# Layer 1 of a two-layer attention and expert kernel: values and routed rows go through the result bank, and both transposed results are one item

## The reference, cut to what matters

```
x = x + cross_attention_0(layernorm(x), ctx, Wq, bq, Wk, bk, Wv, bv, Wo, bo)   # with rotary positions
x = x + experts_0(layernorm(x))                                                # every token, top 8 of 64 experts
x = x + cross_attention_1(layernorm(x), ctx, Wq, bq, Wk, bk, Wv, bv)           # no positions, no output product
x = x + experts_1(layernorm(x))                                                # top 8 of 64, capacity per expert
```

## Time and profile before

| | us |
|---|---|
| median of 3 runs | 2026.81 |
| lowest, highest | 2024.23, 2028.75 |
| the profiled execution | 2026.57 |
| its span, first to last instruction | 2024.9 |
| PE / DVE / ACT / POOL busy, share of the span | 81% / 70% / 61% / 49% |

### The profile page before, as it was taken

How to read it: one execution, slowest core, us unless ns; L and a number is a source line. 1 busy time by engine, 2 the same in 40 slices (tenths; PEclk the granted TensorE clock), 3 DMA queues, 4 the chain that set the end, 5 groups by cost and what they waited for, 6 DMA issues and landing times. The chain is left out here.

```text
span 2024.9 us, 44338 instructions
## 1 busy us (share of the span) xinstructions
PE 1633.4 (81%) x12470; PEld 1095.1 (54%) x12623; DVE 1412.4 (70%) x4341; ACT 1236.0 (61%) x3174; POOL 989.1 (49%) x1114
## 2 busy tenths in 40 slices
PE   3999999999965999999997378888888888855551
PEld 1555555555534888998886134444444444444430
DVE  5888899999954455554434589999999999743330
ACT  1777777777752566666664378778778777621110
POOL 4367777777772000000001776666666662158883
PEclk9999999999987999999998699999999999969995
DMA  5689888787757966666665678887777785178756
GB/s 139 170 211 246 240 220 221 220 220 220 213 169 219 293 202 201 199 203 194 198 197 161 171 191 220 231 219 194 201 198 191 198 199 144 43 200 188 174 94 110
DMA packets 413085, 390.94 MB, mean 193 GB/s; under 512 B 46640, under 2 KB 385072, under 8 KB 412848
## 3 DMA queue, kind: packets, MB, share of 16 engines
q1 hardware_dynamic: 346496, 265.28, 49.4%
q0 software_dynamic: 37904, 90.22, 16.8%
q10 hardware_dynamic: 28448, 32.59, 5.6%
HBM read 233.74 MB, written 170.16 MB: 199 GB/s over the span
## 5 line engine op out<-in xcount | busy, mean ns | idle before, releaser
L1131 DVE TENSOR_REDUCE mx<-psS 128x2 f32<-128x512 f32 x1024 | 678.1, 677 | 88.1 <-PE psS L1525 60.2
L929 ACT ACTIVATE prob<-psE 128x512 f32<-128x512 f32 x1024 | 592.9, 593 | 220.3 <-PE psE L1538 202.5
L778 POOL DMA_INDIRECT yg<-y_d,row_all x256 | 249.5, 975 | 627.5 <-SPq L417 478.6
L1538 PE MATMUL psE<-q,k 128*128 128x256 bf16 x2048 | 393.1, 274 | 35.9 <-ACT prob L929 12.5
L1525 PE MATMUL psS<-k,q 128*128 128x512 bf16 x871 | 336.0, 387 | 28.8 <-DVE mx L1131 14.5
L1477 DVE TENSOR_TENSOR hid<-sil,psE 128x96 f32<-128x96 f32 x384 | 97.7, 254 | 330.5 <-ACT sil L1030 330.5
L1658 PE MATMUL psE<-wt,xgT 128*128 (+1 forms) x1536 | 324.0, 334 | 1.2 <-ACT xgT L1025 0.4
L765 POOL DMA_INDIRECT xs_d<-xr,row_all x256 | 252.1, 985 | 119.9 <-ACT prob L929 75.3
L1538 PEld LDWEIGHTS psE<-q,k 128*128 128x128 bf16 x2048 | 187.3, 98 | 187.4 <-ACT prob L929 59.4
L1556 PE MATMUL psO<-prob,v 128*32 128x256 f32 x4096 | 274.1, 385 | 0.0
L1025 ACT COPY xgT<-psS 128x256 f32<-128x256 f32 x384 | 144.5, 376 | 185.9 <-PE psS L1652 159.6
(11 more groups left out here) (222 smaller groups left out, 2523.8 us busy)
## 6 DMA issues: line engine op xcount, KB each, us to landing
xg<-xs_d SPq DMA_DIRECT2D x320, 128.0 KB, 2.5
y_d<-y_all SPq DMA_DIRECT2D x320, 128.0 KB, 2.3
q<-q_stack_d SPq DMA_DIRECT2D x128, 256.0 KB
k<-k_stack_d SPq DMA_DIRECT2D x128, 256.0 KB
wt<-in_gu ACTq DMA_DIRECT2D x110, 192.0 KB, 3.1
q_stack_d<-parts SPq DMA_DIRECT2D x64, 192.0 KB
k_stack_d<-parts SPq DMA_DIRECT2D x64, 192.0 KB
wt<-in_dn ACTq DMA_DIRECT2D x110, 96.0 KB, 3.8
```

Of the source, the lines that this page charges most:

```text
L778: g.indirect_dma_start(yg[:, k, :], None, y0_d[:, :], bass.IndirectOffsetOnAxis(row_all[:, row(st.pair("load") * K + k, 1)], 0))\
L929: a.activation(prob[gr][:, u % 4, :], psE[ring][:, :], ACT.Exp, scale=SCALE).then_inc(s_exp, 1)
L1131: v_.tensor_reduce(mx[b][:, bg // 4, :].rearrange("p (h r) -> p h r", h=2)[:, :, (bg % 4) * 2 + tt], psS[(UNITS * (st.s0 - LAG["smax"]) + ...
L1538: ins = m_.matmul(psE[ring][:, i * T:(i + 1) * T], k2[b][:, bg, hh * T + i * P:hh * T + (i + 1) * P], q2[b][:, bg, :], start=True, stop=True)
```

## The change

The table of layer 1 gets a third bank, number 2, which is the result bank psO. V and XT move to it; K moves from bank 1 to bank 0, LG from bank 0 to bank 1; OT0 and OT1 become one item OT of four transposes in bank 1, as layer 0 has it. Layer 0's table stays.

In layer 1 these move between units: V on TensorE from 3 to 4; K from 4 to 5; XT from 10 to 5; OT from 5 and 6 to 6; NT from 8 to 9; mT0 from 9 to 10. On ScalarE xr goes from 8 to 4, the copy of XT from 11 to 5, the high part of mT0 from 9 to 10. On VectorE both reciprocals stand in unit 6 and both normalising products in unit 7, the sum x1 goes from 8 to 9, the low part of mT0 from 10 to 11. An item on psO waits until both halves of the result before have been copied out (semaphore s_oev), and the first `values` product of a step waits until V and XT have been copied out of psO (s_v, s_xT).

```diff
@@ MISC, layer 1
-    (("mT1", "attn", 0), ("RK", "place", 1), ("V", "smax", 0), ("K", "front", 1), ("OT0", "back", 0),
-     ("OT1", "back", 1), ("Q", "front", 0), ("NT", "back", 1), ("mT0", "smax", 0), ("XT", "route", 1),
-     ("LG", "route", 0), ("LIST", "post", 1)),
+    (("mT1", "attn", 0), ("RK", "place", 1), ("V", "smax", 2), ("K", "front", 0), ("XT", "route", 2),
+     ("OT", "back", 1), ("Q", "front", 0), ("NT", "back", 1), ("mT0", "smax", 0), ("LG", "route", 1),
+     ("LIST", "post", 1)),
...
@@ bank
-            return psM[at]
+            if at == 2 and st.on("back"):
+                pe.wait_ge(s_oev, st.n("back", 2))
+            return small[at]
+
+        small = [*psM, psO]
...
@@ ScalarE
-                    if u == (10, 11)[L] and st.on("route"):
+                    if u == (10, 5)[L] and st.on("route"):
...
-                    if u == (10, 9)[L] and st.on("smax"):
+                    if u == 10 and st.on("smax"):
                         max_rows("smax", 0)
-                    if u == (14 if filled else (4, 6)[L]) and (st.on("front") or st.on("route")):
+                    if u == (14 if filled else 4) and (st.on("front") or st.on("route")):
                         act.wait_ge(s_rstd, 4 * st.roots())
...
-                    if u == (6, 8)[L] and st.on("route"):
+                    if u == (6, 4)[L] and st.on("route"):
...
@@ VectorE
-                    if L == 1 and u == 8 and st.on("back"):
+                    if L == 1 and u == 9 and st.on("back"):
...
-                    if u == (11, 10)[L] and st.on("smax") and not filled:
+                    if u == 11 and st.on("smax") and not filled:
                         split_max("smax", 0)
...
-                    if u == (7, 5)[L] and st.on("back"):
+                    if u == (7, 6)[L] and st.on("back"):
                         invert(0)
-                    if u == (7, 6)[L] and st.on("back"):
-                        if L == 0:
-                            invert(1)
+                        invert(1)
+                    if u == 7 and st.on("back"):
                         normalise(0)
-                        if L == 1:
-                            invert(1)
-                    if u == 7 and st.on("back"):
                         normalise(1)
...
@@ TensorE, values
+                    if st.L == 1 and q == 0:
+                        if st.on("smax"):
+                            pe.wait_ge(s_v, st.n("smax"))
+                        if st.on("route"):
+                            pe.wait_ge(s_xT, st.n("route"))
...
@@ TensorE, units
-                    if u == 4 and st.on("front"):
+                    if u == (3, 4)[L] and st.on("smax"):
+                        b = st.buf("smax")
+                        product("V", "smax", [(d_ctx[b], st.nbuf("smax"))],
+                                [(ctx_t[b][:, i * P:(i + 1) * P], wbd[L]["v"][:, :]) for i in range(2)], s_vp, P)
+                    if u == (4, 5)[L] and st.on("front"):
                         b = st.buf("front")
                         product("K", "front", [(d_ctx[b], st.nbuf("front"))],
                                 [(wbd[L][n][:, :], ctx_t[b][:, :]) for n in ("ks", "k")[L]], s_kp)
-                    if u == 3 and st.on("smax"):
...
+                    if L == 1 and u == 5 and st.on("route"):
+                        rows_of_x(st)
+                    if u == 6 and st.on("back"):
                         pe.wait_ge(s_oev, st.n("back", 2))
                         ps = bank(pe, st, "OT")
...
-                    if L == 1 and u in (5, 6) and st.on("back"):
-                        h = u - 5
-                        product(f"OT{h}", "back", [(s_oev, st.n("back", 2))],
-                                [(osb[:, half, h * P:(h + 1) * P], None) for half in range(HALVES)], s_ot[h])
-                    if u == (9, 8)[L] and st.on("back"):
+                    if u == 9 and st.on("back"):
                         product("NT", "back", [(s_nrm[0], st.n("back")), (s_nrm[1], st.n("back"))],
                                 [(nrm[:, h, :], None) for h in range(2)], s_ntp)
-                    if u == (10, 9)[L] and st.on("smax"):
+                    if u == 10 and st.on("smax"):
                         product("mT0", "smax", [(s_max, st.n("smax", UNITS, 8))],
                                 [(mx[st.buf("smax")][:, 0, :], None)], s_mT[0])
```

More of the change, by code:

```diff
@@ L438, in lastbuf @@
             return st.nbuf(stage, per) - per
-        FREE = dict(mT0=s_mlo[0], mT1=s_mlo[1], V=s_v, OT=s_nrm[1], OT0=s_nrm[0], OT1=s_nrm[1], Q=s_qr, K=s_kr,
+        FREE = dict(mT0=s_mlo[0], mT1=s_mlo[1], V=s_v, OT=s_nrm[1], Q=s_qr, K=s_kr,
                     NT=s_nt, WO=s_x1, XT=s_xT, LG=s_logit, RK=s_tot, LIST=s_list)
@@ L465, in head_cols @@
         def head_cols(L, h, o, n):
-            tile = psM[item_bank(L, ("OT", f"OT{h}")[L])]
-            first = (h, 0)[L] * 2 * P
+            tile = small[item_bank(L, "OT")]
+            first = h * 2 * P
             return tile[:, first:first + 2 * P].rearrange("p (h r) -> p h r", r=HALF)[:, :, o:o + n]
@@ L915, in max_rows @@
                         act.wait_ge(d_max[h][before.buf(stage)], before.nbuf(stage, 32))
-                    a.copy(mhi[h][:, :], psM[item_bank(L, f"mT{h}")][0:16, 0:P]).then_inc(s_mhi[h], 1)
+                    a.copy(mhi[h][:, :], small[item_bank(L, f"mT{h}")][0:16, 0:P]).then_inc(s_mhi[h], 1)
                 filled = L == 1 and st.s0 == FULL - 2
@@ L940, in body @@
                         wait(act, s_rem, last(st, "front", back=NB))
-                        ps = psE[0] if filled and i == 0 else psM[item_bank(1, "QK"[i])]
+                        ps = psE[0] if filled and i == 0 else small[item_bank(1, "QK"[i])]
                         a.activation(qk[b][:, i, :], ps[:, 0:T], ACT.Identity,
@@ L951, in body @@
                         wait(act, s_wo, last(st, "back"))
-                        a.activation(nt[:, :], psM[item_bank(0, "NT")][:, 0:T], ACT.Identity,
+                        a.activation(nt[:, :], small[item_bank(0, "NT")][:, 0:T], ACT.Identity,
                                      bias=bias[:, 7:8]).then_inc(s_nt, 1)
@@ L998, in body @@
                         wait(act, s_ex, last(st, "route"))
-                        a.copy(logit[:, :], psM[item_bank(L, "LG")][:, 0:E]).then_inc(s_logit, 1)
+                        a.copy(logit[:, :], small[item_bank(L, "LG")][:, 0:E]).then_inc(s_logit, 1)
                     if u == (15 if filled else 13) and st.on("front"):
@@ L1137, in split_max @@
                     dve.wait_ge(s_mhi[h], st.n(stage))
-                    v_.tensor_tensor(mlo[h][:, :], psM[item_bank(L, f"mT{h}")][0:16, 0:P], mhi[h][:, :], ALU.subtract)\
+                    v_.tensor_tensor(mlo[h][:, :], small[item_bank(L, f"mT{h}")][0:16, 0:P], mhi[h][:, :], ALU.subtract)\
                       .then_inc(s_mlo[h], 1)
                 def invert(h):
-                    dve.wait_ge(s_ot[1 if L == 0 else h], st.n("back"))
+                    dve.wait_ge(s_ot[1], st.n("back"))
                     ch.add(v_.reciprocal(rec[:, h, :], head_cols(L, h, 8, 1).rearrange("p h o -> p (h o)")), f"rec{h}")
@@ L1157, in rotate @@
                     b = st.buf("front")
-                    ps = psM[item_bank(0, "QK"[i])]
+                    ps = small[item_bank(0, "QK"[i])]
                     dve.wait_ge((s_qp, s_kp)[i], st.n("front"))
@@ L1222, in body @@
                         now, left = (tally[(st.s0 - LAG["place"] + i) % 2] for i in range(2))
-                        v_.tensor_tensor(now[:, :, :], psM[item_bank(L, "RK")][:, 0:2 * E].rearrange("p (h e) -> p h e", h=2),
+                        v_.tensor_tensor(now[:, :, :], small[item_bank(L, "RK")][:, 0:2 * E].rearrange("p (h e) -> p h e", h=2),
                                          left[:, 1:2, :].broadcast_to((P, 2, E)), ALU.add).then_inc(s_tot, 1)
@@ L1309, in body @@
                         wait(dve, d_x1[b], lastbuf(st, "back"))
-                        v_.scalar_tensor_tensor(x1[b][:, :], psM[item_bank(0, "WO")][:, 0:T], bias[:, 4:5], xres[b][:, :],
+                        v_.scalar_tensor_tensor(x1[b][:, :], small[item_bank(0, "WO")][:, 0:T], bias[:, 4:5], xres[b][:, :],
                                                 ALU.add, ALU.add).then_inc(s_x1, 1)
                     if L == 1 and u == 15 and st.on("post"):
-                        ps = psM[item_bank(1, "LIST")]
+                        ps = small[item_bank(1, "LIST")]
                         dve.wait_ge(s_lsp, st.n1("post"))
@@ L1572, in product, with rows_of_x @@
                     ins.then_inc(done, 1)
+                def rows_of_x(st):
+                    b = st.buf("route")
+                    product("XT", "route", [(s_xr, st.n("route"))],
+                            [(xr[b][:, i * P:(i + 1) * P], None) for i in range(2)], s_xtp)
                 def q_rows(st):
@@ L1600, in body @@
                                 [(wbd[L][n][:, :], ctx_t[b][:, :]) for n in ("ks", "k")[L]], s_kp)
```

(12 more changed lines are left out.)

10 lines of the change are left out of this document (3 added, 7 removed).

## The result

| | before | changed |
|---|---|---|
| median | 2027.78 us (4 runs) | 2005.49 us (4 runs) |
| lowest, highest | 2024.23, 2032.04 | 2001.72, 2007.01 |
| the profiled execution | 2026.57 | 2007.01 |
| its span | 2024.9 | 2005.3 |

The ratio is 0.9886, 95% interval 0.9862 to 0.9911: 22 us faster by the medians, 19.6 between the two profiled executions, where 25.8 were forecast. The time of 2005.5 lies 4.5 us above the 2001 of the forecast. The same kernel beside a second set of runs (experiment 8) gave 0.9891, 0.9876 to 0.9905.

What follows compares the result with a forecast made beforehand. VectorE was taken as the bound, with only its idle time before the reductions of units 4 and 8 to win. 2026.6 - 27.0 - 1.5 + 2.7 = 2000.8, forecast as 2001 us; range 1994 to 2018.

Steps and rivals of the forecast that it cites:

- The two stalls, 27.0 us: VectorE's waits before the reductions of units 4 and 8 go: 1.00 us a step in 27 steps, 27.0 us.
- 49 of 50: Sign that the forecast is right: VectorE busy 49 of 50 us in a window of attention 1.
- The split: Gain per step by stall: 0.37 us before the reduction of unit 4, 0.63 before that of unit 8.
- Fill and drain, -1.5 us: Filling and emptying steps of attention 1: 1.5 us won of the 5.8 us of waits there.
- second stalls: VectorE's 0.55 us wait before the reduction of unit 8, in steps 6 to 32, expected to go.
- what is late next at unit 5: V behind ScalarE's copy of the result delays the scores of unit 5, but they stay covered by 0.3 us.
- rival D: VectorE's stalls only move, to units 5 and 6, so nothing is won: 2024 to 2029 us; chance 0.06.
- The new stall at unit 8, +2.7 us: Q waits for a later xn, delaying the reduction of unit 8: 0.1 us a step, bounds 0 and 0.2.
- The store, 0: Storing mlo costs nothing: about 3.1 us left, landing taken near 2.1; bounds 0 and 0.6 us a step.
- rival A: The store of mlo becomes the new wait, 0.5 to 0.6 us a step lost: about 2016 us; chance 0.15.
- Rivals A, B and C: Rival A; B: the unit 8 stall stays, about 2015 us, 0.08; C: store landing 5.6 us after issue, 2065 us, 0.06.

Runs made afterwards that it cites:

- experiment 8: The changed kernel itself run again beside a second set of runs of the kernel before: 2006.59 us, ratio 0.9891.
- experiment 1: Kernel before with only V moved, to unit 4 and psO: 2021.86 us, ratio 0.9969. Its marks: low part in unit 3 of step 7 to step 9.
- experiment 4: Changed kernel with mT0, and so the store of the low part, one unit earlier on all three engines: 2006.03 us, ratio 0.9899.
- OT alone: Kernel before with only OT0 and OT1 made one item OT, reciprocals in unit 6, products in unit 7: 2013.70 us, ratio 0.9935.
- experiment 3: Kernel before with V on psO in unit 4 and one item OT, but XT and xr left where they were: 2010.07 us, ratio 0.9909.
- experiment 7: Changed kernel with mT0, and so the store of the low part, two units later except in the last filled step: 2017.95 us, ratio 0.9959.
- experiments 3 to 6: Experiment 3, experiment 4, the changed kernel with V one unit later (2008.96 us), and that with mT0 one unit earlier as well (2008.78 us).

## Why the prediction was right, point by point

*The two stalls, 27.0 us.* Right in mechanism and size. Undisturbed steps went from 19.08 to between 18.06 and 18.11 us, VectorE to 99.6% where 49 of 50 was named, and experiments 1 to 3 show the two waits apart. The split was off: 0.37 and 0.63 were foreseen, alone they gave 0.28 and 0.46, and the rest only together.

*Fill and drain, -1.5 us.* This is the term that failed. The emptying steps gave 2.2 us, about what was asked of them. The filling stretch was to get shorter, by its share of this term and by three of the 27 second stalls (1.9 us); it took 96.95 and 96.82 us in two traces, against 95.38 in the one of before. Of the 6.2 us missing between the profiled executions, 3 to 5 are here. The step at fault is the one on what is late next at unit 5: its cover of 0.3 us was worked out in a full step and taken for all. In step 7 VectorE has fewer instructions (no tally stands before the reduction of unit 4), reaches the reduction of unit 5 sooner, and stands 1.01 us for it:

```profile
1208.98 0.69 DVE L1135 TENSOR_REDUCE mx<-psS 128x2 f32<-128x512 f32 x1 [1.01 <-PE psS L1525]
```

Step 8 has the same, 0.98 us. Steps 7 and 8 by the marks of experiment 1 show whose it is, since they come again within 0.03 us in three traces with V and XT where the change puts them (33.29, 33.31, 33.32; experiments 4 and 8 are two of them):

| kernel | steps 7 and 8, us | the filling stretch ahead of them, us |
|---|---|---|
| before | 32.60 | 62.78 |
| V alone | 34.78 | 65.56 |
| OT alone | 31.49 | 65.05 |
| changed | 33.29, 33.32 | 63.66, 63.50 |

OT's part won its two second stalls, V's part cost 1.8 to 2.2 us. That was rival D's mechanism, at unit 5, in the place where its condition held. The cost is the change's own for 0.7 of the 1.5 us. The rest lies ahead, where OT alone took 2.3 us longer with V unmoved, and where the changed kernel was 0.67 us behind by step 5 already, when no V waits for osb yet; this rest is not explained, and with one usable trace of before it can be chance.

*The new stall at unit 8, +2.7 us.* Did not come. From the tally, xn ended 3.19 us later (1409.27 to 1412.46), where the forecast had 3.75 (1413.10 to 1416.85). ScalarE was 0.35 us ahead at osb already (0.67 us before the tally, 0.32 in the earlier trace rows), where I had allowed up to 0.2. In experiment 3, with xr and XT in their later units, it was 0.43 us before the tally, so 0.24 of this is their move.

*The store, 0.* Right: no scores of either trace of the changed kernel wait for it. In most steady steps it lands 1.7 us after its issue (experiment 7) and not at the 2.1 taken from a larger store; the 3.1 us left were more than enough. In 11 steps of experiments 3 to 6, and in crowded ones of experiment 7, scores waited until 2.8 to 4.5 us after the issue, so rival A's mechanism exists, but only the delay of experiment 7 made it cost time that could be seen. The rule of the Trainium skill that was weighed ("DMA: Bandwidth & Descriptors", "Queues, rings and completion order") is borne out by no run: it would fit the crowded steps, but weight loads from ScalarE are under way there too, and none sets the two apart. Rivals A, B and C are out as forecasts for the whole stage.

*Steps 13 to 15.* They lost 2.7 us more than before in the first trace and 1.9 in the second, a cost that the forecast has no term for. In the first, step 13 lost 1.0 us behind a late ScalarE (experiment 4), step 14 lost 0.8 by a mask that waited for GpSimd (below), and step 15 lost 1.6. There two reductions stood 0.54 and 0.55 us for scores, in a stretch in which TensorE's granted clock fell from 1.00 (1349 to 1351 us) to a mean of 0.54 (1351 to 1353) and 0.61 (to 1355), most of it at the lower level, 1.2 GHz; `values` took 1.88 us for 1.07. TensorE had been busy 1.04 of the 2.00 us before. In the second trace the clock stayed at 1.00 and step 15 lost 1.8 us, 0.91 of it at the reduction of unit 5 behind V and 0.5 in the long hotr. That is rival D's mechanism again: where ScalarE's copy comes late, V behind it makes the reduction of unit 5 late. The missing stall of unit 8 made good for most of this.

## What to carry to other kernels

When the engine that sets the end waits for another, which waits for it, take that wait off and price it by the idle time in the bracket: 0.84 of the 1.00 us was that. A cause is not read from a bracket alone: the one of 2.71 us named TensorE, and it was ScalarE's own issue. Count the cover of a moved wait separately in steps that are only half filled and in steps where the engine that is waited for now can be late: a cover worked out in an undisturbed full step is not there. A gain read from one trace holds for its condition: where TensorE's results came 1.4 us later, a kernel with this change was no faster than before.

## What the runs showed of the hardware

An instruction of VectorE with two operands in SBUF that started while GpSimd ran its product of 128x512 on SBUF ended only after it. The mask, 0.23 us otherwise, in the changed kernel:

```profile
1348.00 1.15 POOL L828 TENSOR_TENSOR parts<-rem,parts 128x512 bf16<-128x512 f32 x1 [0.73 <-ACT parts L1007]
...
1348.21 1.02 DVE L1351 TENSOR_TENSOR mask<-rest,logit 128x64 bf16<-128x64 f32 x1
```

It ends at 1349.23, the product at 1349.15. The same befell the sums ys (1.53 for 0.67 us), x (0.91 for 0.40) and hotr (1.71 for 1.22), in each of six traces at one or more places. With an operand in PSUM, or one operand only, nothing happens, in the kernel before for instance:

```profile
1406.95 1.17 POOL L824 TENSOR_TENSOR parts<-rem,parts 128x512 bf16<-128x512 f32 x1 [1.24 <-ACT parts L1003]
...
1407.94 0.20 DVE L1317 SCALAR_TENSOR_TENSOR id_acc<-psM,id_acc 128x64 f32<-128x64 f32 x1
```

That addition started inside such a product 24 times in this trace and took 0.20 or 0.21 us each time. Nor did a small product of GpSimd hold VectorE up. In the changed trace 24 masks started inside one of 128x2 and took 0.22 or 0.23 us:

```profile
1404.39 0.72 POOL L798 TENSOR_TENSOR rstd<-ve,power 128x2 f32<-128x2 f32 x1
...
1404.80 0.23 DVE L1351 TENSOR_TENSOR mask<-rest,logit 128x64 bf16<-128x64 f32 x1
```

By the Trainium skill, "SBUF — State Buffer", section "Who interferes with whom", a VectorE instruction with two SBUF inputs contends with a GpSimd instruction that reads SBUF, and one with at most one SBUF input, outside the modes that take both ports, doesn't. The traces agree for the products of 128x512; beside those of 128x2, which read SBUF too, no wait shows. A change that shifts one engine against the other can so win or lose 0.8 us in a step with no dependence between them.

The issue of a weight load on ScalarE took 0.33 to 0.52 us in 66 of 72 cases of three traces (before, and the two of the changed kernel; steps 10 to 15). Once in each it took 1.86 to 2.19 us, and ScalarE's next exponential started 0.04 or 0.05 us after it had ended. Why these took longer is open.
